# A graph network on one core: one-operand builds of one-hots and permutation, keys loaded earlier, one wait for a selection

## What is computed

```
h = relu(layernorm(x)); x = x + log_softmax(gcn2(relu(gcn1(h))))
gcn:  out = segment_sum((h @ W)[src] * dinv[src] * w * dinv[dst], dst) + self loop + b
h = relu(layernorm(x)); aggr = segment_sum(relu(h[src] + edge_attr @ We + be), dst)
x = x + relu(batchnorm(relu((h + aggr) @ W1 + b1) @ W2 + b2))
```

## Time and profile before

| | |
|---|---|
| median of 3 runs | 6833.05 us (6832.8 to 6845.23) |
| profiled execution, its own time | 6837.09 us |
| its span | 6835.3 us |
| busy: PE, PEld, DVE, ACT, POOL | 4903.3, 3453.0, 4190.3, 1301.4, 4310.2 us |
| indirect DMAs on POOL (L654) | 3476, 4147.2 us, mean 1193 ns |
| masks, one-hots, weighting (L1599, L1563, L1568) | 3040, 1173 and 782 instructions |
| permutation parts (L1658); a mask (L1599) | 608, mean 1215 ns; mean 304 ns |
| chain that ended last, by engine | PE 36%, POOL 32%, issue 14%, DMA 7%, DVE 5% |

### The profile page before, as it was taken

How to read it: one execution, slowest core, us unless ns; L and a number is a source line. 1 busy time by engine, 2 the same in 40 slices (tenths; PEclk the granted TensorE clock), 3 DMA queues, 4 the chain that set the end, 5 groups by cost and what they waited for, 6 DMA issues and landing times.

```text
span 6835.3 us, 117843 instructions
## 1 busy us (share of the span) xinstructions
PE 4903.3 (72%) x29893; PEld 3453.0 (51%) x29894; DVE 4190.3 (61%) x9222; ACT 1301.4 (19%) x4287; POOL 4310.2 (63%) x3554
## 2 busy tenths in 40 slices
PE   4456656565565656559999999976777777787786
PEld 4344434344443434356666666654555555555554
DVE  3666666666666666647778787775444544454453
ACT  4110101111111111141111111133222222222223
POOL 2588888888888888846666666655444444444444
PEclk6677776777777777759999999968988999999997
DMA  1111111111111111122222222232221212122224
GB/s 45 43 39 36 40 37 39 37 39 37 39 38 38 38 39 39 36 52 46 45 46 45 45 46 45 46 98 49 51 49 48 49 47 49 48 49 49 48 49 98
DMA packets 239972, 316.91 MB, mean 46 GB/s; under 512 B 69264, under 2 KB 175179, under 8 KB 239546
## 3 DMA queue, kind: packets, MB, share of 16 engines
q0 software_dynamic: 111232, 170.85, 12.6%
q1 hardware_dynamic: 128688, 145.48, 7.3%
HBM read 276.92 MB, written 39.15 MB: 46 GB/s over the span
## 4 chain that ended last, share of the span: by engine, by line
PE 36%; POOL 32%; issue 14%; DMA 7%; DVE 5%; SPq 2%; ACT 2%; POOLq 0%; ACTq 0%; DVEq 0%
POOL rows_g L654 31%; PE psum L1216 22%; PE psum L1136 7%; DMA x_tab<-sorted_keys 6%; PE psum L1123 3%; DVE rows_g L1613 2%; PE psum L1080 1%; SPq L579 1%; PE psum L1118 1%; ACT rows_g L886 1%; PE psum L1283 1%; DMA rows_g<-table,idx 1%; SPq L585 1%; DVE x_tab L1622 1%; ACT x_more L883 0%
## 5 line engine op out<-in xcount | busy, mean ns | idle before, releaser
L654 POOL DMA_INDIRECT rows_g<-table,idx x3476 | 4147.2, 1193 | 2222.0 <-ACT idx L789 1129.5
L1216 PE MATMUL psum<-x_tab 125*128 x8512 | 1360.3, 302 | 81.9 <-issue 46.1
L1136 PE MATMUL psum<-hot,rows_g 128*96 128x128 f32 x7512 | 1111.8, 303 | 257.1 <-DMA rows_g<-table,idx 196.3
L1159 PE MATMUL psum<-x_tab 128*104 128x512 bf16 x2432 | 743.4, 442 | 672.5 <-DVE x_tab L1658 652.0
L1136 PEld LDWEIGHTS psum<-hot,rows_g 128*96 128x96 f32 x7512 | 993.7, 184 | 385.5 <-issue 262.8
L1216 PEld LDWEIGHTS psum<-x_tab 125*128 125x128 bf16 x8512 | 858.3, 101 | 612.2 <-issue 186.9
L1576 DVE TENSOR_TENSOR acc<-acc,psum 96x128 f32 x1173 | 328.9, 280 | 1103.6 <-PE psum L1136 1095.2
L1613 DVE TENSOR_REDUCE rows_g<-psum 128x384 f32<-128x1152 f32 x304 | 412.5, 1357 | 846.5 <-PE psum L1216 846.5
L787 ACT ACTIVATE attr<-edge 128x12 f32 (+1 forms) x1173 | 245.8, 211 | 3466.5 <-PE psum L1136 3463.6
L1159 PEld LDWEIGHTS psum<-x_tab 128*104 128x104 bf16 x2432 | 304.2, 143 | 1043.7 <-DVE x_tab L1658 522.5
L1658 DVE TENSOR_TENSOR x_tab<-x_tab 128x2048 bf16<-128x2048 f16 x608 | 708.6, 1215 | 0.0
(11 more groups left out here) (256 smaller groups left out, 4076.6 us busy)
## 6 DMA issues: line engine op xcount, KB each, us to landing
rows_g<-table,idx POOLq DMA_INDIRECT x3476, 2.6
x_tab<-sorted_keys SPq DMA_DIRECT2D x304, 125.0 KB
x_more<-in_edge_attr_dram SPq DMA_DIRECT2D x238, 64.0 KB
sorted_attr<-x_tab SPq DMA_DIRECT2D x38, 384.0 KB
x_more<-sorted_attr SPq DMA_DIRECT2D x152, 96.0 KB
table<-x_tab SPq DMA_DIRECT2D x13, 840.0 KB
x_tab<-in_edge_attr_dram SPq DMA_DIRECT2D x38, 256.0 KB, 2.8
x_tab<-in_x_dram SPq DMA_DIRECT2D x2, 4200.0 KB
```

What stands on the lines that cost most here:

```text
L654: pool.indirect_dma_start(out=rows_g[u][0:np_, g * F:(g + 1) * F], out_offset=None, in_=table[p], in_offset=bass.IndirectOffsetOnAxis(ap=i ...
L1136: last = pe.matmul(ps_agg[t.b], rows_g[t.u][0:t.np_, g * F:(g + 1) * F], hot[t.h][0:t.np_, g, :], start=g == 0, stop=g == G - 1)
L1159: last = pe.matmul(ps_perm[b], ship[:, c, :], perm[c % 3][:, b * BK:(b + 1) * BK], start=c == 0, stop=c == SC - 1)
L1216: last = pe.matmul(ps_sel[c], mask[i % 2][j][:, c * P:(c + 1) * P], tab3[:, bass.ds(w[c] + j, 1), :, :].rearrange("q a k f -> q (a k f)"), ...
```

## The change

Four edits. (1) `build_hot` in passes one and two is four TENSOR_SCALAR instructions, one for each column, that compare and multiply in one, instead of two TENSOR_TENSOR over all columns; pass three keeps its one TENSOR_TENSOR. (2) `sort_perm` is a TENSOR_SCALAR that takes the rank as a per-partition scalar; the float16 copy of the ranks (L1653) and its link are gone. (3) In pass three SP loads the key two selections ahead, and the edge attributes of `Gather` 4 and 5 one phase earlier. (4) `select` waits once for all ten masks, signals once, and takes its block as `w[c]` of a view that starts at j.

```
-        rank_h = at_tab.take(SC * 16, F16).rearrange("p (c k) -> p c k", k=16)
...
             def load_iter(it):
                 for i in range(NP):
-                    for k in ((0, 1, 2), (3,), (4,), (5,))[i]:
+                    for k in ((0, 1, 2), (3, 4), (5,), ())[i]:
                         t = Gather(it, k)
                         load_ea(fast, t.gi, t.s, t.h, EP)
-                    sp.wait_ge(s_part3, 6 * NC)
-                    load_key(2, it, i)
+                    if i + 2 < NP:
+                        load_key(2, it, i + 2)
+                    elif not isinstance(it, int):
+                        load_key(2, it + 1, i + 2 - NP)
                     load_eaT3(it, i)
...
             load_z(0)
+            sp.wait_ge(s_part3, 6 * NC)
+            load_key(2, 0, 0)
+            load_key(2, 0, 1)
...
                 pe.wait_ge(s_row, n + 1)
+                pe.wait_ge(s_mask, 2 * KB + (n + 1) * KB)
...
-                    pe.wait_ge(s_mask, 2 * KB + n * KB + j + 1)
                     for c in range(G):
                         last = pe.matmul(ps_sel[c], mask[i % 2][j][:, c * P:(c + 1) * P],
-                                         tab3[:, bass.ds(w[c] + j, 1), :, :].rearrange("q a k f -> q (a k f)"),
+                                         tab3[:, j:J - KB + 1 + j, :, :][:, bass.ds(w[c], 1), :, :].rearrange("q a k f -> q (a k f)"),
                                          start=p == 1 and j == 0, stop=j == KB - 1)
-                    last.then_inc(s_sel, 1)
+                last.then_inc(s_sel, KB)
...
+                rel = attr[t.u][0:np_, 0:G]
+                if p == 2:
+                    last = dve.tensor_tensor(hot[t.h][0:np_, :, :], iota[0:np_, 0:W].unsqueeze(1).to_broadcast([np_, G, W]),
+                                             rel.unsqueeze(2).to_broadcast([np_, G, W]), ALU.is_equal)
+                else:
+                    for g in range(G):
+                        last = dve.tensor_scalar(hot[t.h][0:np_, g, :], iota[0:np_, 0:W], rel[:, g:g + 1],
+                                                 attr[t.u][0:np_, G + g:G + g + 1], ALU.is_equal, ALU.mult)
...
-                link(it, dve.tensor_copy(rank_h, rank[:, :].unsqueeze(2).to_broadcast([P, SC, 16])))
...
-                dve.tensor_tensor(split16(perm[c % 3]), split16(iota_h),
-                                  rank_h[:, c, :].unsqueeze(1).to_broadcast([P, SE // 16, 16]), ALU.is_equal).then_inc(s_perm, 1)
+                dve.tensor_scalar(perm[c % 3], iota_h, rank[:, c:c + 1], None, ALU.is_equal).then_inc(s_perm, 1)
```

More of the change, by code:

```diff
@@ L329, in build_gnn @@
         s_slow3 = sem("slow_attr_loaded")
-        s_hot1 = sem("hot_unweighted")
         s_pay = sem("payload_ready")
@@ L605, in _ @@
                 load_z(it + 1)
-            with sp.Fori(XI - 1, LOOPS) as it:
+            with sp.Fori(XI - 1, LAST) as it:
                 load_iter(it)
+            load_iter(LAST)
             for k in range(REST):
@@ L1622, in split @@
                     dve.tensor_tensor(t, t, tab3[:, js, k, :], ALU.subtract).then_inc(s_left3, 1)
-            LINKS = 14
+            LINKS = 13
             links = [0]
@@ L1652, in sort_rank @@
                 link(it, dve.tensor_tensor(rank[:, :], rank[:, :], dupes[:, :], ALU.add))
-                link(it, dve.tensor_copy(rank_h, rank[:, :].unsqueeze(2).to_broadcast([P, SC, 16])))
             def sort_perm(it, c):
                 dve.wait_ge(s_permd, SC * it + c + 1)
-                split16 = lambda t: t.rearrange("p (a k) -> p a k", k=16)
-                dve.tensor_tensor(split16(perm[c % 3]), split16(iota_h),
-                                  rank_h[:, c, :].unsqueeze(1).to_broadcast([P, SE // 16, 16]), ALU.is_equal).then_inc(s_perm, 1)
+                dve.tensor_scalar(perm[c % 3], iota_h, rank[:, c:c + 1], None, ALU.is_equal).then_inc(s_perm, 1)
             def sort_columns(it):
```

## The result

The changed kernel takes 5768 us (median of 4 runs, 5738.1 to 5793.3) where the kernel before takes 6834; the ratio is 0.844, 95% interval 0.839 to 0.848. The forecast was 5835 us, within 5730 to 6060.

What follows compares the result with a forecast made beforehand. It took POOL to bound pass one, PE pass two, and a loop of waits pass three. From the profiled time, 6837.1 - 462 - 156 - 384 + 3 = 5838 us, against a forecast median of 5835, range 5730 to 6060.

Steps and rivals of the forecast that it cites:

- That is above POOL's 52.5, so PE bounds: Pass one: PE's chain at 56.5 us an iteration exceeds POOL's 52.5, so PE bounds; gain 462 us.
- a part of 0.65 us holds it up three times as long, say 0.25 us: Pass one: each permutation part delays POOL's indirect DMAs 0.25 us, for 8 DMAs, 2 us an iteration.
- The 0.7 us that the forecast adds for the lower clock: Pass one: iteration sum of 55.8 us taken as 56.5, since the last group sometimes runs at the lower clock.
- None over 2 us beside parts: Pass one, sign: indirect DMAs near 1.01 us mean, with none over 2 us beside permutation parts.
- Four selections x 0.4: Pass three: register work saved in four selections, 0.4 us each, 1.6 us an iteration.
- lower clock behind a wait, all but gone: Pass three: PE's lower clock behind a wait, 1 us in most phases, nearly vanishes, gaining 1.7 us an iteration.
- One edge load is still issued behind the join, 0.9 us: Pass three: one edge load, still issued behind the join and needed at the fifth product, keeps 0.9 us of waiting.
- The exponentials were costed at 3 us: Pass three: four exponentials ahead of ACT's copy in phase 0 of 25 iterations keep some 3 us each, 2 on average.
- POOL stays blocked by whole trains: Rival, pass one: trains of TENSOR_SCALAR still block POOL, which needs 62 us an iteration; 209 us more, 6045 us; chance 0.13.
- Another load takes the key's place: Rival, pass three: edge or sorted attributes become the wait, half the 384 us is lost, 6025 us; chance 0.13.
- Parts that get no faster: Rival, pass one: permutation parts stay at 1.14 us, 6 of the 12 us are lost, 6065 us; chance 0.05.
- a clock that falls: Rival, passes two and three: idle PE's clock falls to 1.2 GHz, +1900 us, 7735 us; chance 0.02.

Runs made afterwards that it cites:

- the control: The changed kernel with all four edits, unaltered, in a second comparison with the kernel before: 5788 us against 6829, ratio 0.848.
- the first profile: The first profiled execution of the changed kernel, all four edits against the kernel before: 5793.3 us.
- all three: Changed kernel with exponentials at the end of ACT's phase 1, the z_part load behind edge loads and key, pass one's one-hots as two TENSOR_TENSORs: 5607 us.
- the pieces: The kernel before with each permutation part made by four TENSOR_TENSORs of 512 columns instead of one of 2048, on another chip: 7919 us, ratio 1.016.
- long parts: The changed kernel with the permutation part reading its column numbers as float32 instead of float16, on another chip: 7222 us, ratio 0.928 to the kernel before.
- the exponentials' first run: The changed kernel with ACT's four exponentials moved to the end of phase 1 in 25 iterations of pass three, on another chip: 7111 us.

## Why the forecast held, point by point

Against its own profiled sum, 5838 us, the profiled execution came out 45 lower: pass one 1.25 x 38 = 48 better, pass two 0.2 x 38 = 8 better, pass three 0.4 x 38 = 15 worse, 4 left over. The durations read from neighbouring rows were good: parts 0.66 us apart (0.65), four one-hots 1.10 (1.05), a selection 5.28 (5.2), 12 products of a group 2.79 (2.6), a group 4.8 (4.6), and the gaps of pass two 8.7, 7.0, 6.9, 10.5 (8.6, 6.7 to 6.8, 6.7 to 6.8, 10.7). The bounds of the passes were named rightly, that of pass one by a margin far smaller than foreseen. Four steps behind these sums were off all the same.

- **"That is above POOL's 52.5, so PE bounds."** PE does, with the chain at 54.4 to 56.5 us in the control, near the 56.5 taken. But the margin over POOL, foreseen as 4 us, is 0.6 (54.9 against 55.5), and in the first profile POOL is on the chain that ended last in some 17 of 37 iterations. The term that was too small is "a part of 0.65 us holds it up three times as long, say 0.25 us", with the one-hots 2.6 us an iteration: indirect DMAs were held up (1.077 - 0.947) x 40 = 5.2 us. It cost little only since the chain of PE was a little longer still. The 0.7 us that the forecast adds for the lower clock fall on the first three-part group, not on the last.
- **"None over 2 us beside parts."** 61 were. The kernel with the permutation edit alone had none. In the changed kernel those held start 0.1 to 0.5 us ahead of a train and end 0.12 us behind it; one that starts within 0.4 us behind the train's start ends 0.15 us behind the second part. This is read from the records of the 190 trains. With the permutation edit alone some 75 start 0.3 us ahead of a train and none is held, so why some are held through two ends and others not stays open.
- **"Four selections x 0.4".** The term is there, but something else takes it back. Beside the key edit, only the select edit touches pass three. In the 13 iterations without exponentials, the key edit alone gives 40.53 us and all four 38.57: 1.96 us less, where 1.6 was foreseen. In the 25 with exponentials it is 45.51 against 46.64, though PE's waits in gap 3-0 are alike (3.1 and 3.0 us). What differs is the granted clock, in gap 1-2 0.98 with the key edit alone and 0.90 with all four, in gap 3-0 0.94 and 0.84. The 12 products behind the wait for ACT's copy, first with the key edit alone (after 3.29 us of waiting), then in the control (after 3.12):

```profile
5249.30 1.64 PE L1222 MATMUL psum<-x_tab 125*128 x12
```
```profile
4566.39 3.09 PE L1220 MATMUL psum<-x_tab 125*128 x12
```

  So the forecast's "lower clock behind a wait, all but gone" failed in those two gaps, and why the shorter stream lowers the clock there isn't shown. Whoever adds single gains counts 1210 us; the forecast escaped most of that since its terms were made against the bound of each pass, not against the kernel before.
- **"One edge load is still issued behind the join, 0.9 us."** The wait was 2.2 us in 24 iterations. With the load of `gcn_out` moved behind the edge loads it is gone (all three), and 1.2 us of waiting for ACT's copy are left in its place. The exponentials were costed at 3 us; PE's wait is 3.1, but gap 3-0 shrank by 3.9 when they went, for in the control the products behind the wait are slow too.

**The rivals.** "POOL stays blocked by whole trains" is true of one DMA in 24 in pass one and no more; the pieces show that with TENSOR_TENSORs it stays so when each is cut in four. (The page named there speaks of one instruction, not of a train.) "Another load takes the key's place" happened on a small scale (2.2 us in one of four phases, 24 times of 38). Parts that get no faster, and a clock that falls, didn't happen: the granted clock is 0.99 in pass two (before 1.00) and rose from 0.91 to 0.94 in pass three.

## What to carry to other kernels

When GpSimd issues gathers, count what VectorE does beside them by kind: on this kernel a TENSOR_TENSOR train held a gather to its last end, also when cut in four, and one tensor operand with a per-partition scalar mostly let it through; with parts of 0.74 us instead of 1.22, that was worth 562 us of 6831 alone. An engine that never pauses isn't thereby the bound: POOL is as full after the change as before, and PE waits for it no longer or hardly. Where several engines are near the bound of a stretch, measure the gap between two fixed events in each phase: it shows at once which edits need each other (gap 0-1). Comparing whole iterations shows which take each other's gain (pass one). A wait that moves its name without moving the time, as from ACT's copy to the edge load, says that a queue's order is the next edit.

## What the runs showed of the hardware that was not expected

**Waits that never wait cost PE's stream 0.8 us in 40 products**, nine waits and nine signals, some 90 ns for each pair; together with the additions they kept 40 products of 288 columns at 162 ns each instead of 132.

**One operand of 16 bits.** The part as TENSOR_SCALAR takes 0.744 us from float16 and 1.276 from float32, as TENSOR_TENSOR 1.215. The Trainium skill (VectorE: DVE Perf Modes, the perf-mode tier table) has 693 ns for a `tensor_scalar` of 2048 bfloat16 elements, 1227 for one of float32 and 1224 for a `tensor_tensor` of bfloat16; the trace agrees within 8%.

**Another chip.** On it the kernel before took 7787 us instead of 6831, and the variants of the changed kernel 7111 to 7224. In each iteration of all three passes there is one place where PE's instructions come in ones and twos, with no releaser; in pass two it lies in gap 0-1, which is 18.6 us there instead of 8.6. From the exponentials' first run:

```profile
4024.44 0.29 PE L1221 MATMUL psum<-x_tab,x_more 125*128 x1 [0.29 <-issue]
...
4027.96 0.40 PE L1221 MATMUL psum<-x_tab,x_more 125*128 x1 [0.96 <-issue]
```

It looks like instructions that arrive late behind the loop's jump, and no run tested it. Pieces and long parts were run on that chip alone.
